# Selective scan on one core: the sum over 16 states kept in two tiles by DMA accumulation instead of one

## The reference

```
h = layernorm(x) * (1 + ca) + sa
z = h @ W_in; val, gate = split(z)
u = silu(conv3(val))                      # depthwise, along the tokens
B, C = u @ W_B, u @ W_C                   # 16 states each
Delta = softplus((u @ W_delta + delta_base) @ W_tau)
A_bar = exp(Delta * A); B_bar = expm1(Delta * A) / (Delta * A + 1e-6) * Delta * B
h_t[n] = A_bar[n] * h_(t-1)[n] + B_bar[n] * u_t      # for each of 16 states n
y_t = sum over n of h_t[n] * C_t[n]
x = x + ga * (y * silu(gate) @ W_out + h)
h = layernorm(x) * (1 + cb) + sb
x = x + gb * (top-2 of 8 experts(h) + shared expert(h))   # gelu(h @ W1 + b1) @ W2 + b2
```

## Time and profile before

| | us |
|---|---|
| median of 3 runs | 4697.77 |
| lowest, highest run | 4693.6, 4699.59 |
| the profiled execution | 4694.18 |
| its span, first to last instruction | 4692.4 |
| granted clock of PE, mean of the core | 0.888 of full speed |

### The profile page before, as it was taken

The page is one execution under the profiler, slowest core; times in us unless marked ns, Lnnn a source line. Parts: engine busy times, 40 slices in busy tenths (PEclk is TensorE's granted clock), DMA queues, the critical chain, the costliest instruction groups (busy, mean ns, idle before and its releaser), DMA issues.

```text
span 4692.4 us, 37024 instructions
## 1 busy us (share of the span) xinstructions
PE 3849.1 (82%) x9708; PEld 1612.3 (34%) x9708; DVE 4033.8 (86%) x3896; ACT 3945.9 (84%) x4282; POOL 3647.7 (78%) x2304
## 2 busy tenths in 40 slices
PE   6623413999899899989998998999998987988889
PEld 3201101333343333333343333333333333333344
DVE  1288899999999999999999999999999997887820
ACT  1698898998989898999989898989999897887811
POOL 0399987887889888888889888888888896767721
PEclk7856656999999999999999999999999988989889
DMA  3589867888888888888888888898988876657542
GB/s 131 197 247 266 236 170 198 238 235 255 231 253 233 257 246 258 232 251 248 242 255 234 254 235 258 236 267 221 264 252 236 238 210 166 192 154 196 138 146 67
DMA packets 352220, 1037.18 MB, mean 221 GB/s; under 512 B 41253, under 2 KB 44389, under 8 KB 344710
## 3 DMA queue, kind: packets, MB, share of 16 engines
q1 hardware_dynamic: 278282, 766.35, 47.9%
q0 software_dynamic: 73728, 268.47, 29.0%
HBM read 639.74 MB, written 126.51 MB: 163 GB/s over the span
## 4 chain that ended last, share of the span: by engine, by line
ACT 21%; PE 19%; DMA 13%; POOL 13%; issue 13%; DVE 8%; POOLq 0%; SPq 0%; DVEq 0%; ACTq 0%
DMA ysum<-hs 13%; PE ps L1125 7%; PE ps L1144 6%; POOL inv L1390 4%; POOL hs L1363 3%; ACT inv L761 3%; ACT th L772 3%; PE ps L1095 3%; ACT inv L767 3%; ACT abar L776 2%; ACT inv L754 2%; DVE ps L1191 2%; DVE ps L1179 2%; POOL ysum L1377 2%; DVE ps L1185 2%
## 5 line engine op out<-in xcount | busy, mean ns | idle before, releaser
L1390 POOL TENSOR_TENSOR inv<-inv,th 128x1024 f32<-128x1024 f32 x512 | 1268.0, 2477 | 148.8 <-ACT th L772 146.5
L1125 PE MATMUL ps<-hf,w1r 128*128 128x512 f32 x2304 | 1104.0, 632 | 38.6 <-ACT hid L884 23.3
L1363 POOL TENSOR_TENSOR hs<-hs,Cb 128x1024 f32<-128x1024 f32 x384 | 977.3, 2545 | 30.1 <-DVE hs L1209 13.2
L1162 PE MATMUL ps<-Brow,pick 48*128 48x512 bf16 x1024 | 346.6, 422 | 630.2 <-DVE hs L1209 629.1
L1144 PE MATMUL ps<-w2r,hid 128*128 128x512 f32 x1776 | 812.1, 604 | 0.8 <-ACT xn L884 0.7
L754 ACT ACTIVATE inv<-nrd,kappa 128x1024 f32<-128x1024 f32 (+1 forms) x640 | 578.6, 967 | 201.5 <-DVE ps L1191 197.4
L1179 DVE SCALAR_TENSOR_TENSOR ps<-ps,us 128x1024 f32<-128x1024 f32 x512 | 628.0, 1227 | 134.0 <-PE ps L1162 133.5
L1377 POOL DMA_DIRECT2D ysum<-hs x480 | 442.6, 922 | 367.4 <-DMA ysum<-hs 356.9
L1191 DVE SCALAR_TENSOR_TENSOR ps<-ps,inv 128x1024 f32<-128x1024 f32 x512 | 627.9, 1226 | 81.0 <-POOL inv L1390 59.2
L1198 DVE SCALAR_TENSOR_TENSOR ps<-nrd,inv_kappa,ps 128x1024 f32<-128x1024 f32 (+1 forms) x640 | 675.2, 1073 | 15.8
L1209 DVE TENSOR_TENSOR_SCAN hs<-abar,carry,ps 128x512 f32<-128x512 f32 (+1 forms) x384 | 683.5, 1801 | 0.3
(11 more groups left out here) (154 smaller groups left out, 5021.2 us busy)
## 6 DMA issues: line engine op xcount, KB each, us to landing
ysum<-hs POOLq DMA_DIRECT2D x512, 512.0 KB, 5.7
Cb<-c_rows SPq DMA_DIRECT2D x384, 512.0 KB, 4.6
w1r<-in_W SPq DMA_DIRECT2D x144, 512.0 KB, 5.3
w2r<-w_scaled SPq DMA_DIRECT2D x141, 512.0 KB, 8.1
Cb<-c_rows SPq DMA_DIRECT2D x128, 256.0 KB, 4.0
gbc<-expert_gates SPq DMA_DIRECT2D x128, 256.0 KB, 5.4
aw<-in_W_val SPq DMA_DIRECT2D x64, 256.0 KB, 6.3
xa<-in_x SPq DMA_DIRECT2D x32, 512.0 KB, 7.2
```

The lines of the kernel that those rows point to most:

```text
L1125: mm = t.matmul(o, w1r[:, n % 2, k, h * P:(h + 1) * P], hf[:, k, :], start=(k == 0), stop=(k == G - 1))
L1363: gp_.tensor_tensor(hs[:, c % 4, :], hs[:, c % 4, :], Cb[:, c % 2, :], ALU.mult).then_inc(hC_done, 1)
L1390: gp_.tensor_tensor(inv[:, c % 6, :], inv[:, c % 6, :], th[:, c % 3, :], ALU.mult).then_inc(thinv_done, 1)
```

## The change

`ysum` becomes two tiles, one for the even and one for the odd states, with a semaphore each. The first state of each kind is a plain copy, the others are added; each transfer waits for the last but one. The four buffers of h stay, and the scan of state c waits for the sum that took state c - 4. At the end of a unit POOL adds the two tiles (one more tensor_tensor of 128x1024, semaphore `y_joined`) ahead of the gating multiply. `add_to_y(c - 1)` moves ahead: it now stands right behind `times_C(c - 1)`, except in slots 1 and 17, where it stays behind `gate_y`.

For the second tile's room `hid` gives up a place: the sixth hidden tile (place 5 of 6, expert product 5 of 9) lies in the first half of `uu`, the tile of u; ACT waits there until u has been stored and B and C have been computed from it, and the next tile's value product waits until the W2 products have read it. The folds have three stages instead of four; the third part of the modulation weights is loaded into `hs`, and the halo tokens into `th`. b2's scaling on DVE stands four slots later (c + 2 in place of c + 6).

```diff
-        ysum = sb("ysum", [P, TB])
+        ysum = sb("ysum", [P, 2, TB])
-        hid = sb("hid", [P, HB - 2, HT, T])
+        hid = sb("hid", [P, HB - 3, HT, T])
-        stage = [x1[:], hf[:], hidf[:, 0:4 * T].rearrange("p (g t) -> p g t", g=4),
-                 hidf[:, 4 * T:8 * T].rearrange("p (g t) -> p g t", g=4)]
+        stage = [x1[:], hf[:], hidf[:, 0:4 * T].rearrange("p (g t) -> p g t", g=4)]
 
         def hidden(p):
             i = p % HB
-            return xn[:, 2 * (i - 3):2 * (i - 3) + 2, :] if i in (3, 4) else hid[:, i if i < 3 else 3]
+            if i == 5:
+                return uu[:, 0:HT, :]
+            return xn[:, 2 * (i - 3):2 * (i - 3) + 2, :] if i in (3, 4) else hid[:, i]
...
-        y_summed, y_gated, carry_done = sem("y_summed"), sem("y_gated"), sem("carry_done")
+        y_summed = [sem("even_states_summed"), sem("odd_states_summed")]
+        y_joined, y_gated, carry_done = sem("y_joined"), sem("y_gated"), sem("carry_done")
...
                     ge(act, mm_bc, q)
+                    if has(q - 5):
+                        act.wait_ge(mm_w2, 12 * (q - 5) + 8)
...
                     ge(act, mm_w2, hid_free(q, e))
+                    if e % HB == 5 and has(q + 4):
+                        act.wait_ge(st_u, 16 * (q + 5))
+                        act.wait_ge(mm_bc, q + 5)
...
                     if c >= 4:
-                        dve.wait_ge(y_summed, 16 * (c - 3))
+                        dve.wait_ge(y_summed[c % 2], 16 * (c // 2 - 1))
...
-            if 0 <= c + 6 < 2 * NF * NB and (c + 6) % (2 * NF) == 0:
-                b = (c + 6) // (2 * NF)
+            if 0 <= c + 2 < 2 * NF * NB and (c + 2) % (2 * NF) == 0:
+                b = (c + 2) // (2 * NF)
...
                     pool.wait_ge(hC_done, c + 1)
-                    if c % N == 0:
+                    if c % N < 2:
                         ge(pool, y_gated, unit(c))
-                        gp_.dma_start(ysum[:], hs[:, c % 4, :]).then_inc(y_summed, 16)
+                        gp_.dma_start(ysum[:, c % 2, :], hs[:, c % 4, :]).then_inc(y_summed[c % 2], 16)
                     else:
-                        pool.wait_ge(y_summed, 16 * c)
-                        gp_.dma_start(ysum[:], hs[:, c % 4, :], accum_op=ALU.add).then_inc(y_summed, 16)
+                        pool.wait_ge(y_summed[c % 2], 16 * (c // 2))
+                        gp_.dma_start(ysum[:, c % 2, :], hs[:, c % 4, :], accum_op=ALU.add).then_inc(y_summed[c % 2], 16)
...
-                    pool.wait_ge(y_summed, 16 * N * (u + 1))
+                    for odd in range(2):
+                        pool.wait_ge(y_summed[odd], 16 * (N // 2) * (u + 1))
+                    gp_.tensor_tensor(ysum[:, 0, :], ysum[:, 0, :], ysum[:, 1, :], ALU.add).then_inc(y_joined, 1)
+                    pool.wait_ge(y_joined, u + 1)
                     pool.wait_ge(gate_ld, 16 * (u + 1))
-                    gp_.tensor_tensor(gy[:], ysum[:], gy[:], ALU.mult).then_inc(y_gated, 1)
+                    gp_.tensor_tensor(gy[:], ysum[:, 0, :], gy[:], ALU.mult).then_inc(y_gated, 1)
...
             times_C(c - 1)
+            if r not in (1, 17):
+                add_to_y(c - 1)
...
             if r in (1, 17):
                 gate_y(c // N - 1)
-            add_to_y(c - 1)
+                add_to_y(c - 1)
```

More of the change, by code:

```diff
@@ L175, in col @@
             return modc[:, m * G + g, b:b + 1]
-        wmod_h = [inv[:].rearrange("p s t -> p (s t)")[:, 0:2 * G * D], abar[:].rearrange("p s t -> p (s t)"), hidf[:, 0:2 * G * D]]
+        wmod_h = [inv[:].rearrange("p s t -> p (s t)")[:, 0:2 * G * D], abar[:].rearrange("p s t -> p (s t)"),
+                  hs[:].rearrange("p s t -> p (s t)")]
         wdT = flat(x1[:]).rearrange("p (k n) -> p k n", k=G)
@@ L184, in adaln_mamba_moe @@
         halo = gy[:, 0:G * 2 * NQ].rearrange("p (g i) -> p g i", g=G)
-        hx = hs[:, 0, 0:D]
+        hx = th[:, 0, 0:D]
         mrow = w2r[:].rearrange("p e h d -> p (e h) d")
```

## The result

The changed kernel takes 4712.11 us (median of 6 runs, 4704.03 to 4715.0) against 4695.69 us of the kernel before, measured beside it (6 runs, 4691.41 to 4699.59). The ratio is 1.0034, with a 95% interval from 1.0021 to 1.0047: **slower, by 16 us** (0.3%), where 4697 us and "no difference" were forecast. The profiled execution took 4704.03 us, the lowest of its runs; its span is 4702.1.

A forecast was written before the change was run, and what follows sets the result against it. No single bound: DVE in first halves, DVE and ACT in second, POOL in the last ten slots of 12 windows. From 4694.2, minus 4 (setup) plus 6 (those stretches) gave 4696; stated 4697 us, range 4655 to 4745.

The forecast's parts named there:

- Part (1): POOL's accumulating transfers into two tiles: DMA waits vanish, 356.9 us of idle in the run, 6.0 per bound stretch.
- Part (2): Transfer right behind hs*C: POOL waits for its own multiply, taken as 0.55 us a slot, between 0.41 and 0.68.
- the lower end of the range (0.13): Lowest price considered for POOL's wait on hs*C, from the copy of the carry: 0.13 us with the overlap.
- the first alternative (0.41): Cheaper wait for hs*C, 0.41 us a slot, if the accumulating transfer saves 0.27 behind a self-wait.
- Part (3): At unit ends, POOL adds the two tiles: 32 joins of 2.5 us, 80 in all, mostly beside other work.
- Part (4): Setup and buffers: three stages, modulation weights in hs, halo in th, sixth W1 tile in u's buffer: cost nothing.
- Part (5): Setup, b2's product on DVE four slots later: its store waits go, POOL's added work offsets; gain 4 us.
- Part (6): Last ten slots of 12 windows: 5.5 us of waits against 6.0 removed, join adds about 1; +6 us total.
- cheap self-wait, faster: Rival: the wait on hC_done costs only 0.13 us, so bound stretches and setup gain; 4650 us, chance 0.30.
- POOL becomes the bound: Rival: at 0.97 us a slot, POOL's work outgrows second halves and lengthens setup; 4752 us, chance 0.26.
- the one for the fast side: Sign in the changed profile: POOL's self-wait on hs*C under 0.3 us would show the forecast too slow.
- the one for the slow side: Sign in the changed profile: second halves over 128 us would show the forecast too fast.

The follow-up runs named there:

- e7: The kernel before, with only the small edge operation moved from DVE to POOL; 4694.85 us, ratio 1.0003.
- e10: e4 with b2's product back at c + 6, four slots earlier, against e4; 4665.39 us.
- e4: The changed kernel with the transfer back behind the weight and the edge operation on POOL; 4647.72 us, ratio 0.9897 to the kernel before.
- e2: The changed kernel with the edge operation moved from DVE to POOL's slot 4, same sum; 4666.14 us.
- e3: The changed kernel with the transfer back behind the weight, two tiles kept and the edge operation on DVE; 4685.16 us.
- e8: The kernel before with only the moves of memory and ACT's added waits; 4700.39 us, ratio 1.0003.
- e5: The changed kernel with DVE's edge operation as a reduction over an axis of one, halo left out; 4667.9 us.
- e11: e5 plus a DVE tensor_scalar, SBUF to SBUF, right behind the edge operation, for which nobody waits; 4706.32 us.
- e12: The kernel before plus an unused DVE tensor_scalar, SBUF to SBUF, in slot 12 of each window; 4700.94 us, ratio 1.0015.
- e1: The changed kernel with DVE's edge operation as a one-input multiply by one, halo left out; 4709.1 us.

## Why the prediction was wrong

The runs form a chain of steps from the one kernel to the other, by medians:

| step | us | difference |
|---|---|---|
| edge operation on POOL, nothing else (e7) | 4694.85 | 0 |
| + two tiles behind the weight, memory moves (e10) | 4665.39 | -29 |
| + b2 four slots later (e4) | 4647.72 | -18 |
| + transfer in front of the weight, with its wait for hs*C (e2) | 4666.14 | +18 |
| + edge operation back on DVE (the change) | 4712.11 | +46 |

The differences add up to +17 by construction. Each time in the chain is known to about 6 us, so a difference to about 9. The shares also depend on the order: with the transfer behind the weight, the edge operation on DVE costs 37 (e3 against e4), and the transfer's place costs 27 while that operation is on DVE (the change against e3). **The change gives 47 us, takes back 18 through its own wait, and loses 46 to an operation that its diff does not touch.**

- *Part (1), the DMA waits vanish*: right; 17.8 us of the join's remain over the whole run of the 356.9. With the joins and the moves of memory in it, the step is worth 29 us (e10 against e7). The prediction saw 12 x 6.0 = 72 us of wait there and a cap of 41 us by DVE.
- *Part (2), the wait for hs*C*: it is there, 446 times where some 480 were forecast, but at 0.33 us, not 0.55 (146 us in all, not 250 to 330); the lower end of the range (0.13) was below it, the first alternative (0.41) above. Behind the gate, from where the price was taken, the wait is still 0.58 in the mean after the change (18.0 us in 31); behind hs*C it is another price. The prediction's reading that the gap is longer where POOL's instructions overlap does not hold in the kernel before: the seven overlapping gates have a median of 0.58 like the 24 clean ones. The 0.1 us of the Trainium skill's "DMA: Bandwidth & Descriptors" (section on the anatomy of one DMA), which the prediction set beside it, stands there for the semaphore update at the end of a DMA, and not for an engine's wait for its own instruction: it was no price for this wait, and is too low by 0.23 where mine was too high by 0.22.
- *Part (3), the joins*: 32 for 76 us on POOL, forecast 80; that they lie beside other work was not tried alone.
- *Part (4), memory*: nothing, as said (e8).
- *Part (5), b2 and the setup*: forecast 4 us earlier at the end of the setup, seen 5.2. Right in the sum and wrong in the parts, so partly luck: b2's place alone is worth 18 (e10 against e4) instead of being nearly eaten by 24 us of waits; these are 12.1 us in 37 between 230 and 623, and with them unit 3 begins 12 us later (e2 against e4).
- *Part (6), the bound stretches*: this is **the step that failed**. It went by POOL alone and let all else stand: "first halves unchanged at 131 to 133 us". They are at 134.9, and bring 12 x 2.4 = 29 us, while the second halves, costed at +0.5 each, fell by 1.1, minus 14. Together with the setup that is +10, which is the distance of the two profiled executions (4704.03 and 4694.18). What was missing is a term: a transfer's wait was costed for what POOL does not do in it, and not for what DVE can do meanwhile. The runs put in its place the edge operation, 29.1 us in 16 instead of 6.4, which costs 44 to 46 us (e5, e2).
- *The sum*: that 4697 lies only 15 us below the measured time is luck, since two errors cancel in part. With 0.33 in place of 0.55, the prediction's own sums give about 4660, an estimate (12 x (6.0 - 3.3 - 1.0) = 20 us from the bound stretches and 14 from the setup, off 4694), near the 4666 to 4668 that were measured without the held operation; the self-wait's price made the forecast some 30 us too slow, and the missing term 44 to 46 too fast. Besides, 4696 and the 3.6 between median and profiled execution make 4700, not the 4697 that was said.
- *The rivals*: "cheap self-wait, faster" had the mechanism half right. Without the held operation the change takes 4666 to 4668 us (e2, e5), where it said 4650. "POOL becomes the bound" fell: DVE's wait for POOL went down, over the whole run from 59.2 to 42.0 us. The slowdown came by a way that stood in no rival. Of the marks that the prediction set itself, the one for the fast side (a wait under 0.3 us) and the one for the slow side (second halves over 128 us) were both missed; DVE's busy time was not among them.

What stays open: 26.5 us less of DVE's busy time (29.1 to 2.6, the change to e5) brought 44 us. A part is seen in the traces: from 640 to 4450 us DVE's wait for PE's products with B (L1187 on L1170) is 133.6 us in the change and 123.9 in e5, since PE gets its bank from DVE's scan and starts later behind a held DVE. 26.5 + 9.7 = 36 of the 39 us between the two profiled executions. This was read, not tried.

## What to carry to other kernels

A wait on one engine can be another's shelter. Before a change takes idle time out of GpSimd, list the operations of VectorE that it can hold (two inputs in SBUF, or a tensor_scalar from SBUF to SBUF; both were held here), see in the timeline whether GpSimd is idle when they run, and price each at one to two of GpSimd's instructions if it no longer is. Such an operation, if small, belongs on GpSimd itself (0.3 to 0.5 us here), or in a form that is not held. And compare the durations of instructions that the diff does not touch: an engine's busy time that grows with no instruction added is the first row to chase.

## What the runs showed of the hardware

An operation of DVE that is held does not get in between two multiplies of POOL that overlap by 0.3 us. In the change b2's product, 0.68 us by itself, took 5.06 us (DVE, then POOL):

```profile
291.95 5.06 DVE L1225 TENSOR_TENSOR w2r<-bc_sb,gbc 9x512 f32<-9x512 f32 x1
297.04 1.23 DVE L1199 SCALAR_TENSOR_TENSOR ps<-ps,inv 128x1024 f32<-128x1024 f32 x1
...
291.51 2.64 POOL L1401 TENSOR_TENSOR inv<-inv,th 128x1024 f32<-128x1024 f32 x1
293.82 2.62 POOL L1442 TENSOR_TENSOR hf<-hf,gbc 128x1024 f32<-128x1024 f32 x1
296.12 0.92 POOL L1367 COPY carry<-hs 128x2 f32<-128x2 f32 x1
```

It came 0.44 us after the start of POOL's first multiply. At that one's end (294.15) it did not get in: the second multiply's row begins 0.33 us earlier. It ended at 297.01, which is its own 0.68 us after 296.33, just ahead of the second multiply's end (296.44). The copy of the carry, whose row overlaps the second multiply by 0.32, did not hold it. The 103 held operations of this kind (the edge's, b2's and the added ones of e11 and e12) in all 14 traces read alike: each ends its own free length, less 0.12 us, after the end of an instruction of POOL, to within 0.02. In 21 of them the end of a multiply passed first without letting them in, and there the next multiply's row overlapped it by 0.32 to 0.35. Where the next was the copy, or an instruction that overlapped by less than 0.1, they got in (57 times).

The Trainium skill's "SBUF — State Buffer" (section "Who interferes with whom") speaks of the whole of one instruction; these rows, and the 3.15 us at 2088.61, go over more than one. So the worst price is not one instruction of 2.6 us but a run of them, up to 4.96 us for eight columns in e1. In six rows the held operation begins up to 0.45 us ahead of the multiply (2607.01 against 2607.46 in e11), while POOL issues a transfer; what holds it in that part is not shown. From the other side, the same eight columns take 0.16 us when free, and as a reduction (e5) they were free 16 times of 16.

The wait of POOL for its own last instruction showed as 0.30 us in most cases (at 2092.03 and 3597.24), whether that instruction overlapped the one before it or not. About one in ten took 0.5 to 0.9 (0.67 at 3541.36), and why is not shown. Behind the gate's multiply it is 0.58 in the mean. One number for "a wait for oneself" doesn't exist in this trace; take it from the same pair of operations.
